# Second of three attentions through one pipeline: the key and query products moved to the start of a step, the turn of the largest scores moved one step earlier

## The reference

```python
q_in = layernorm(x)
src  = (ctx @ W_src.T + b_src) * mask[:, None]     # 128 x 256: keys, values
tgt  = (q_in @ W_tgt.T + b_tgt) * mask[:, None]    # 128 x 128: queries
k, v = split(src);  q = tgt                        # 8 heads of 16
scores = q @ k.T / 4;  scores[:, mask == 0] = -inf
attn = softmax(scores);  upd = attn @ v
x = x + tanh(g) * (concat(q_in, upd) @ W_out.T + b_out)
```

## Time and profile before

| | us |
|---|---|
| three timed runs | 1160.93, 1164.42, 1164.43 |
| median | 1164.42 |
| span of the profiled execution, first to last instruction | 1125.8 |
| PE busy in the span | 916.2 (81%) |
| DVE busy | 662.2 (59%) |
| ACT busy | 437.8 (39%) |
| POOL busy | 437.6 (39%) |
| granted PE clock, mean over the span | 0.884 |

### The profile page before, as it was taken

The page is one execution under the profiler, slowest core; times in us unless marked ns, Lnnn a source line. Parts: engine busy times, 40 slices in busy tenths (PEclk is TensorE's granted clock), DMA queues, the critical chain, the costliest instruction groups (busy, mean ns, idle before and its releaser), DMA issues.

```text
span 1125.8 us, 23576 instructions
## 1 busy us (share of the span) xinstructions
PE 916.2 (81%) x8435; PEld 731.0 (65%) x8435; DVE 662.2 (59%) x1745; ACT 437.8 (39%) x864; POOL 437.6 (39%) x718
## 2 busy tenths in 40 slices
PE   2867796999974988995777859999578888887898
PEld 2555685888863766774556638988446666666565
DVE  3788744876765555433354525756755777653565
ACT  0444535333323232321454315566403445555312
POOL 4444445444611554225455343647243353200100
PEclk9988757999995999996899659999856999999999
DMA  5311113112222000001122101123111000001262
GB/s 173 106 52 56 57 48 97 37 40 54 65 59 78 15 15 10 1 1 69 57 72 68 35 24 48 44 60 79 36 33 37 25 26 22 17 8 29 73 202 83
DMA packets 51310, 59.34 MB, mean 53 GB/s; under 512 B 7456, under 2 KB 36928, under 8 KB 50816
## 3 DMA queue, kind: packets, MB, share of 16 engines
q1 hardware_dynamic: 45776, 46.44, 13.5%
q0 software_dynamic: 4992, 10.23, 4.0%
q10 hardware_dynamic: 432, 1.18, 0.3%
HBM read 42.81 MB, written 9.24 MB: 46 GB/s over the span
## 4 chain that ended last, share of the span: by engine, by line
PE 59%; DVE 18%; issue 6%; DMA 6%; POOL 4%; ACT 4%; SPq 2%; POOLq 0%; DVEq 0%; ACTq 0%
PE banks L412 10%; DVE NM L482 6%; PE bank L181 4%; PE banks L420 4%; PE banks L175 3%; PE banks L177 3%; PE banks L176 3%; PE banks L1813 3%; PE bank L433 3%; PE bank L2235 3%; PE banks L1814 3%; PE banks L1816 3%; PE banks L1815 3%; PE bank L2126 2%; DMA QT<-NMT 2%
## 5 line engine op out<-in xcount | busy, mean ns | idle before, releaser
L412 PE MATMUL banks<-KT,QT 31*128 31x128 f32 (+1 forms) x1280 | 160.6, 386 | 95.1 <-DVE NM L482 38.0
L482 DVE TENSOR_REDUCE NM<-banks 128x4 f32<-128x1024 f32 (+1 forms) x112 | 136.7, 1220 | 142.7 <-PE banks L412 142.5
L412 PEld LDWEIGHTS banks<-KT,QT 31*128 31x128 f32 x1280 | 113.1, 223 | 133.2 <-DVE NM L482 48.5
L456 ACT ACTIVATE EE<-banks 128x1024 f32<-128x1024 f32 x112 | 114.6, 1024 | 191.8 <-PE banks L420 191.5
L420 PE MATMUL banks<-QT,KT 32*128 32x128 f32 x1792 | 155.8, 316 | 3.7 <-ACT EE L456 3.1
L420 PEld LDWEIGHTS banks<-QT,KT 32*128 32x128 f32 x1792 | 128.6, 214 | 7.6 <-issue 4.5
L1745 POOL DMA_INDIRECT XG<-xn,SL x92 | 89.0, 968 | 100.3 <-PE bank L1783 80.5
L433 PE MATMUL bank<-EE,VV 128*32 128x128 f32 x1792 | 72.0, 306 | 1.1 <-ACT EE L456 1.0
L1882 ACT ACTIVATE ONE<-CP,EC 128x128 fp32r<-128x128 f32 x92 | 37.0, 403 | 79.0 <-PE bank L2065 55.7
L433 PEld LDWEIGHTS bank<-EE,VV 128*32 128x32 f32 x1792 | 52.1, 122 | 13.5 <-issue 10.2
L175 PE MATMUL banks<-HH,W1H 128*128 128x512 f32 x128 | 51.7, 404 | 6.4 <-DVE HH L2591 6.2
(11 more groups left out here) (405 smaller groups left out, 2415.9 us busy)
## 6 DMA issues: line engine op xcount, KB each, us to landing
RAW<-in_w SPq DMA_DIRECT2D x19, 512.0 KB, 3.7
CBS<-cw SPq DMA_DIRECT2D x32, 256.0 KB, 3.5
ys<-Y SPq DMA_DIRECT2D x92, 64.0 KB, 1.5
RAW<-in_w SPq DMA_DIRECT2D x8, 352.0 KB, 3.2
KT<-in_keys SPq DMA_DIRECT2D x8, 256.0 KB, 3.0
KT<-KQ SPq DMA_DIRECT2D x32, 64.0 KB, 1.9
QT<-KQ SPq DMA_DIRECT2D x32, 64.0 KB, 1.9
CTX<-in_ctx SPq DMA_DIRECT2D x3, 512.0 KB, 4.2
```

Of the source, the lines that this page charges most:

```text
L412: ins = pe.matmul(out, self.QT[r, b1 % 4, 128 * g:128 * g + 128], moving(r, 128 * g), start=True, stop=True)
L456: act.activation(self.EE[:, b % 2, 2 * p:2 * p + 2, :].rearrange("p i k -> p (i k)"), self.K.SB[:, :], ACT.Exp).then_inc(sig("ee").sem, 1)
L482: dve.tensor_reduce(out, src, AX.X, ALU.max, negate=True).then_inc(sig("m1").sem, 1)
```

## The change

Nothing is computed differently; instructions move. (1) On PE a step now opens with the key and query products of batch `s`. Their transposes stand in the step before, behind the values (`pe_turns`, called once ahead of the loop). (2) DVE writes `KQ` before it takes the maximum. (3) The largest scores of `b1` = `s-1` are turned, copied and sent in the step in which their maximum is taken, not one step later; on PE that turn comes behind the output product and the turn of the heads. (4) The router's PE work comes last in a step. (5) ACT copies `OT` first, then `FC` and `FT` of batch `s+1`, then takes the exponential, then copies `NMT`. (6) `FT` has 7 buffers in place of 6.

```diff
--- before.py
+++ after.py
@@ -2639,7 +2639,7 @@
         sb = K.sb
         self.XN = sb(st, "XN4", [128, 2, 128])
         self.FC = sb(st, "FC4", [128, 2, 256])
-        self.FT = sb(st, "FT4", [128, 6, 128])
+        self.FT = sb(st, "FT4", [128, 7, 128])
         self.TV = sb(st, "TV4", [128, 2, 128])
         self.KT = sb(st, "KT4", [128, NBAT, 256])
         self.FK = K.DEP
@@ -2671,7 +2671,7 @@
             sp.dma_start(self.KT[row:row + 1, :, :].rearrange("p b (g k) -> p b g k", g=2),
                          self.NEG[:, :].unsqueeze(1).to_broadcast([16, 2, 128])).then_inc(sig("key_masks").sem, 16)
         for s in range(0, self.LAST + 1):
-            b2 = s - 2
+            b1 = s - 1
             if s < NBAT:
                 sp.wait_ge(*sig("kqc")(s + 1))
                 if s >= 4:
@@ -2680,8 +2680,8 @@
                     sp.wait_ge(*sig("qc")(1))
                 H.sp_rows(self.KT[0:128:2, s, :], self.KQ[:, s % 2, 0, :], sig(f"keys_in{s % 4}").sem)
                 H.sp_queries(s, self.KQ[:, s % 2, 1, :])
-            if 0 <= b2 < NBAT:
-                H.sp_largest(b2)
+            if 0 <= b1 < NBAT:
+                H.sp_largest(b1)
             self.early.sp(s)
 
     def pe(self):
@@ -2689,21 +2689,13 @@
         A, B, C, O = (K.PS[i][:, :] for i in (5, 6, 7, 4))
         ws, wo = K.wt("Wsrc"), K.wt("Wout")
         read_a, read_b, read_c, read_o = [], [sig("quarter")(1)], [], []
+        self.pe_turns(0)
+        read_a = [sig("ft")(1)]
         for s in range(0, self.LAST + 1):
-            b1, b2, b3, b4, b5 = (s - i for i in range(1, 6))
+            b1, b3, b4, b5 = (s - i for i in (1, 3, 4, 5))
             keys = lambda kb, r, c: self.KT[r, b3 % NBAT, c:c + 128]
             moving = lambda r, c: self.KT[r, b1 % NBAT, c:c + 128]
-            fc, f = self.FC[:, s % 2, :], self.FT[:, s % 6, :]
-            for r in read_a:
-                pe.wait_ge(*r)
-            read_a = []
-            if s < NBAT:
-                for i in range(2):
-                    pe.transpose(A[:, 128 * i:128 * i + 128], K.CTX[:, s, 128 * i:128 * i + 128], K.ident)
-                pe.wait_ge(*sig("xn1")(s + 1))
-                pe.transpose(A[:, 256:384], self.XN[:, s % 2, :], K.ident).then_inc(sig("x_turned").sem, 1)
-                read_a.append(sig("ft")(s + 1))
-            H.pe_scores(0, b1, moving, b3, keys)
+            fc, f = self.FC[:, s % 2, :], self.FT[:, s % 7, :]
             if s < NBAT:
                 for r in read_b:
                     pe.wait_ge(*r)
@@ -2712,6 +2704,7 @@
                     pe.matmul(B[:, 0:128], ws[:, 256 * i:256 * i + 128], fc[:, 128 * i:128 * i + 128], start=(i == 0), stop=(i == 1))
                 pe.matmul(B[:, 128:256], K.wt("Wtgt"), f, start=True, stop=True).then_inc(sig("kq").sem, 1)
                 read_b = [sig("kqc")(s + 1)]
+            H.pe_scores(0, b1, moving, b3, keys)
             if 0 <= b4:
                 for r in read_o:
                     pe.wait_ge(*r)
@@ -2723,6 +2716,11 @@
                     ins = H.pe_values(b4, [b4 % 4], 0, 8)
                 ins.then_inc(sig("pv").sem, 1)
                 read_o = [sig("ot")(b4 + 1)]
+            if s + 1 < NBAT:
+                for r in read_a:
+                    pe.wait_ge(*r)
+                self.pe_turns(s + 1)
+                read_a = [sig("ft")(s + 2)]
             for r in read_c:
                 pe.wait_ge(*r)
             read_c = []
@@ -2732,15 +2730,9 @@
                                     start=(i == 0), stop=(i == 1))
                 ins.then_inc(sig("proj").sem, 1)
                 read_c.append(sig("tv")(s + 1))
-            if 0 <= b2 < NBAT:
-                for r in read_a:
-                    pe.wait_ge(*r)
-                H.pe_largest(b2, A[:, 384:512]).then_inc(sig("nm_turned").sem, 1)
-                read_a = [sig("nmt")(b2 + 1)]
-            read_b = self.early.pe(s, read_b)
             if 0 <= b5:
                 pe.wait_ge(*sig("ot")(b4 + 1))
-                pe.matmul(C[:, 128:256], self.FT[:, b5 % 6, :], wo[:, 0:128], start=True, stop=False)
+                pe.matmul(C[:, 128:256], self.FT[:, b5 % 7, :], wo[:, 0:128], start=True, stop=False)
                 pe.matmul(C[:, 128:256], H.OT[:, b4 % 2, 256:384], wo[:, 128:256], start=False,
                           stop=True).then_inc(sig("outp").sem, 1)
                 read_c.append(sig("x_done")(b5 + 1))
@@ -2748,22 +2740,27 @@
                 pe.wait_ge(*sig("ot")(b4 + 1))
                 H.pe_out(b4, C[:, 256:512])
                 read_c.append(sig("on")(b4 + 1))
+            if 0 <= b1 < NBAT:
+                for r in read_a:
+                    pe.wait_ge(*r)
+                H.pe_largest(b1, A[:, 384:512]).then_inc(sig("nm_turned").sem, 1)
+                read_a = [sig("nmt")(b1 + 1)]
+            read_b = self.early.pe(s, read_b)
+
+    def pe_turns(self, s):
+
+        K, sig, pe, A = self.K, self.K.sig, self.K.nc.tensor, self.K.PS[5][:, :]
+        for i in range(2):
+            pe.transpose(A[:, 128 * i:128 * i + 128], K.CTX[:, s, 128 * i:128 * i + 128], K.ident)
+        pe.wait_ge(*sig("xn1")(s + 1))
+        pe.transpose(A[:, 256:384], self.XN[:, s % 2, :], K.ident).then_inc(sig("x_turned").sem, 1)
 
     def act(self):
         K, H, sig, act = self.K, self.H, self.K.sig, self.K.nc.scalar
         A, O = K.PS[5][:, :], K.PS[4][:, :]
+        self.act_features(0)
         for s in range(0, self.LAST + 1):
-            b2, b3, b4, b5 = (s - i for i in range(2, 6))
-            if s < NBAT:
-                act.wait_ge(*sig("x_turned")(s + 1))
-                if s >= 6:
-                    act.wait_ge(*sig("outp")(s - 5))
-                if s >= 2:
-                    act.wait_ge(*sig("proj")(s - 1))
-                act.copy(self.FC[:, s % 2, :], A[:, 0:256])
-                act.copy(self.FT[:, s % 6, :], A[:, 256:384]).then_inc(sig("ft").sem, 1)
-            if 0 <= b3 < NBAT:
-                H.act_exp(b3, 0)
+            b1, b3, b4, b5 = (s - i for i in (1, 3, 4, 5))
             if 0 <= b4:
                 c = slice(0 if b4 < NBAT else 256, 384 if 0 <= b5 else 256)
                 act.wait_ge(*sig("pv")(b4 + 1))
@@ -2772,9 +2769,24 @@
                 if b5 >= 2:
                     act.wait_ge(*sig("outp")(b5 - 1))
                 act.copy(H.OT[:, b4 % 2, c], O[:, c]).then_inc(sig("ot").sem, 1)
-            if 0 <= b2 < NBAT:
-                H.act_largest(b2, A[:, 384:512]).then_inc(sig("nmt").sem, 1)
+            if s + 1 < NBAT:
+                self.act_features(s + 1)
+            if 0 <= b3 < NBAT:
+                H.act_exp(b3, 0)
+            if 0 <= b1 < NBAT:
+                H.act_largest(b1, A[:, 384:512]).then_inc(sig("nmt").sem, 1)
             self.early.act(s)
+
+    def act_features(self, s):
+
+        K, sig, act, A = self.K, self.K.sig, self.K.nc.scalar, self.K.PS[5][:, :]
+        act.wait_ge(*sig("x_turned")(s + 1))
+        if s >= 7:
+            act.wait_ge(*sig("outp")(s - 6))
+        if s >= 2:
+            act.wait_ge(*sig("proj")(s - 1))
+        act.copy(self.FC[:, s % 2, :], A[:, 0:256])
+        act.copy(self.FT[:, s % 7, :], A[:, 256:384]).then_inc(sig("ft").sem, 1)
 
     def dve_rows(self, b, T):
 
@@ -2800,10 +2812,10 @@
         dve.tensor_scalar(self.NEG[:, :], self.F16[:, :], 0.0, NEG, ALU.is_equal, ALU.mult).then_inc(sig("neg").sem, 1)
         for s in range(0, self.LAST + 1):
             b1, b4, b5 = s - 1, s - 4, s - 5
+            if s < NBAT:
+                self.dve_rows(s, B)
             if 0 <= b1 < NBAT:
                 H.dve_max(b1, 0)
-            if s < NBAT:
-                self.dve_rows(s, B)
             if s + 2 < NBAT:
                 K.dve_stats((s + 2) % 4, [K.X[:, s + 2, :]])
             if 0 <= b4 < NBAT:
```

## The result

The changed kernel takes 1126.1 us (median of 4, 1125.05 to 1128.03); the kernel before took 1162.68 with the run beside it: ratio 0.973, interval 0.967 to 0.978. On other occasions the changed kernel was timed beside the kernel before twice more, with 0.967 (0.961 to 0.972) and 0.970 (0.963 to 0.978).

The account below looks back on a forecast made before the run. No engine bound the kernel; a ring of waits through DVE's `KQ` and SP's DMAs did. Start-up 7.7, middle 11.6 and tail 5.3 summed to 24.6 us off 1164.42: 1139.8, said as 1140, range 1132 to 1152.

Parts of the forecast that it names:

- the ring: Middle of `Attn2`: scores, DVE's maximum, `KQ`, SP's issues and the largest scores' landing close in a step's 6.53 us.
- The floor of a step: PE's groups in a step sum to 4.93 us if nothing is late; 5.1 taken for a plain step.
- ACT's ring: Ring through scores, values, transposes, copies and exponential: closes in 5.0 us, practically the same bound as PE.
- the middle: Steps 5 to 15: 62 us against 73.65, -11.6, bounds -14.4 and -6.
- Router's work: Steps 10, 11, 14 and 15: PE work no longer hidden, 3.0 us, and waits for bank 6, 2.0.
- Weights: SP's 512 KB load just ahead of keys may delay queries: 1 us for weights and late queries, at most 4.
- Start-up: First four steps: 22 us taken against 29.73, -7.7, bounds -11 and -4.
- Tail: From step 16: shortened behind the second `BT`, rank 2 us later but regained; -5.3 us, bounds -7 and -2.
- change partner: Rival: ACT's exponential or SP's queue binds instead, steps 5.7 to 6.0 us, total about 1147, 1152 with weak tail; 20%.
- The slower clock: Rival: PE at half clock makes steps 8.1 to 9.7 us, total 1172 to 1190; 5%.

Follow-up runs that it names:

- experiment 2: Kernel before with `KQ` ahead of the maximum, largest scores turned early, or both: plain steps 6.21, 5.99, 5.66 us; changed kernel with both undone: 6.54.
- exp_first: Changed kernel with ACT's exponential ahead of the copies of `OT`, `FC` and `FT`: plain step 4.78 us against 4.67; ratio to the kernel before 0.967.
- experiment 5: The run exp_first, ACT's exponential put first in the changed kernel: plain step 4.78 us in place of 4.67.
- weights_xn_again: Changed kernel with SP issuing the router's weights and rows `xn` ahead of the largest scores, `xn` one step later; second run: middle 55.6 us, ratio 0.965.
- after_again: Changed kernel unchanged, timed again on another occasion: 1093.8 us against 1131.9 for the kernel before.
- experiment 4: Changed kernel with SP issuing weights ahead of the largest scores, also with `xn`: with both, start-up plus middle 75.1 and 74.8 us against 78.5, 79.7 and 80.5.
- experiment 3: Router's PE work moved back ahead of the output product in the changed kernel: tail 40.5 us against 30.1; moved last in the kernel before: 34.3 against 41.5.
- router_before_output: Changed kernel with the router's PE work back ahead of the output product and turn of the heads: tail 40.5 us, ratio to before 0.986.

## Why the forecast was right in direction and too small

- **What bound the kernel, and the ring.** Right, and shown: taking one part out of the ring moved the step by the amount read from the earlier trace rows, and the products' place alone by nothing. That the three together give 4.67 takes PE's own path as well (experiment 2), which the forecast had in its floor.
- **The floor of a step.** Forecast 4.93, took 5.1; measured 4.67. From start to start in the timeline above, transposes took 0.39 (forecast 0.49), projection and turn of `NM` 0.55 (0.67), output and heads 0.67 (0.76), values 0.83 (0.78). Lines of before, beside the earlier trace rows, say where 0.25 of the 0.26 too much come from:

```profile
575.23 0.48 ACT L2774 COPY OT<-bank 128x384 f32<-128x384 f32 x1 [0.44 <-PE bank L433]
576.08 0.39 PE L2744 MATMUL bank<-WS,OT 128*128 128x128 f32 x2
576.74 0.27 PE L2704 MATMUL bank<-CP,XN 128*128 128x128 f32 x1
```

  The 0.49 of the transposes is no start-to-start time: 577.01 is the end of the last one (576.74 + 0.27), while the next instruction follows a single product's start by 0.11 (563.63 to 563.74): 0.16 too much. And the output product stood right behind `OT` (copied by 575.71, L2743 at 575.76): 0.32 to the next start (576.08) against 0.23 (562.96 to 563.19) in the kernel after, where `OT` was ready 0.21 earlier. `exp_first`, which takes that lead away, takes 0.11 longer for a step. The rest moved between groups. The 0.17 put on top for ACT's ring was a bound already covered (experiment 5). 0.43 too much in 11 steps is 4.7 us: this is the mis-sized term of the middle.
- **Router's work.** Forecast 5.0. In `weights_xn_again`, free of late queries, steps 10, 11 and 14 are 6.05, 6.01 and 6.05 and the rest plain: 55.6 less 11 x 4.67 is 4.2. Nearly right; step 15's part fell where a transpose and a projection no longer are.
- **Weights.** Forecast 1 us, at most 4. Middle of after less 51.4 (11 plain steps) and 4.2: 2.7 us, of which 1.6 is step 5 at the lower clock, a term that the sum didn't have. Late queries are the rest, 0.25 in step 8 and 0.92 in step 14; in after_again they are 1.5 us, 0.4 of it behind weights (step 6) and 1.0 in step 9, where the cause is open (experiment 4). So the size was right. By the rule of the Trainium skill that the prediction cites ("DMA: Bandwidth & Descriptors", section "Queues, rings and completion order"), queries land behind the weights. The trace agrees: in after_again weights issued at 550.08 landed at 554.33, and queries issued at 552.42 at 554.69. The start-up has some 2 us of it too, where the forecast had none.
- **Start-up.** Forecast 22, measured 22.2, 21.4 and 21.5. In part luck: the late queries of step 4 weren't in the forecast (6.10 us against 4.38 in `weights_xn_again`), and the clock was 0.76 to 0.85 where the forecast reckoned from 0.68.
- **Tail: the step that failed.** "The rank gets later ... by 2 us, and the places that follow it get it back": no change up to the first `BT`. Counted from the start of step 16, the `BT` started 18.5 us on before and 13.3 after, so 5.1 us were lacking: step 16 1.3 shorter, the way to the rank 0.4 (though the output product now lies on it), the rank 1.7 at full clock, and 1.7 because output product, `ON` and `X` no longer lie between rank and places. The granted clock up to the rank was 1.00 in place of 0.57 and 0.50, so the first three are clock as well as order; by experiment 3 the order alone gave 7.2 of the whole tail. Behind the second `BT` the forecast had 7.3 us to the end (661.8 - 654.46), and 7.3 it was (630.03 to 637.3); that `BT` itself was 4.06 in place of 4.65. (The 654.1 in its sum for `X` is a slip for 654.46.) Of the miss in the tail most is the part declared unchanged.
- **The rivals.** The ring did not change partner on a plain step (4.67 against 5.7 to 6.0); the queue did, in single steps. The slower clock came only in step 5 of two of the three profiles: 0.97 in the middle.
- **The range.** Its low end was the "best bounds" of three terms, two of which were not bounds: the floor of 4.93 was 0.26 too high, and the tail's took a whole part as fixed.

## What to carry to other kernels

A pipeline's step is the longest of several rings, and edits that shorten it are worth their sum only until the next ring: list every ring with its length, and expect an edit off the longest to give nothing alone and much with the others. To price the step once a processor is the bound, add its groups' times from one start to the next where it doesn't wait, and don't mix in a time that runs to an end. In a tail without overlap, follow the chain from the tail's start, clock included, before anything is called unchanged.

## What the runs showed of the hardware

- Queries (64 KB) issued 1.1 us behind 512 KB on the same queue landed in 4.29 us in place of 1.95, and others issued 1.9 us behind took 2.58.
- The granted clock in the third attention was between 0.78 and 0.85 for one and the same code, which took 245 and 226 us; the routed layer took 139 to 141 or 151 to 153 us at 0.94 to 0.96, with nothing between in 17 profiles, and the same level in all profiles of one occasion after the first. What decides is open.
- PE kept its full clock through steps 16 and 17 and the rank in the kernel after; in `router_before_output`, whose work is the same, it was 1.00 up to 616.3, 2 us into step 17, and 0.50 from there on, before the rank (617.96).
- The second `BT`, the same eight POOL instructions, took 4.64 us in the kernels with the router first and 4.06 in those with it last. In the former DVE's `ON` and `X` of a batch fell wholly beside it, but so they did beside the first `BT` of the kernel after, which took 4.07; the reason is open.
